# First products of an attention kernel 14 steps ahead instead of 12, and its row maxima turned three steps earlier

## The reference

```
q = x @ q_w.T + q_b
xd = depthwise conv over positions, width 3, stride 2 (2048 -> 1024), + conv_b
k = xd @ k_w.T + k_b ;  v = xd @ v_w.T + v_b
att = softmax(q k^T / sqrt(16))           # 16 heads of 16 channels, 2048 x 1024
x = layernorm(x + (att v) @ out_w.T + out_b)
x = layernorm(x + (x + 0.5 * (silu((layernorm(x)*gamma+beta) @ w1 + b1) @ w2 + b2)))
```

## Time and profile before

| | us |
|---|---|
| median of 3 runs | 5294.16 |
| lowest, highest | 5277.87, 5350.97 |
| the profiled execution | 5288.4 |
| its span, first to last instruction | 5286.6 |
| TensorE busy in the span | 4912.2 |
| VectorE, ScalarE busy | 3396.7, 2773.8 |
| mean granted TensorE clock | 0.72 of full |

### The profile page before, as it was taken

One profiled execution on the slowest core, in us unless ns is written; L12 is line 12 of the kernel. 1 busy time (PEld: TensorE's weight loads), 2 busy tenths in 40 slices (PEclk: granted clock), 3 DMA queues, 4 the chain that ended last, 5 costly groups with the idle time before them and its releaser, 6 DMA issues. The chain is left out here.

```text
span 5286.6 us, 93279 instructions
## 1 busy us (share of the span) xinstructions
PE 4912.2 (93%) x30808; PEld 2220.8 (42%) x30808; DVE 3396.7 (64%) x4144; ACT 2773.8 (52%) x4969; POOL 844.1 (16%) x553
## 2 busy tenths in 40 slices
PE   9889999999999999999899999988999998999999
PEld 6523333333333333333233333332333336999998
DVE  9765656566666566556665566565666566777775
ACT  4355555555555555555555555565555564333333
POOL 5402000000000000000000000000000005777776
PEclk9976666666765667556756566676666679999999
DMA  9921031003100400040004000400130012222221
GB/s 309 292 44 47 22 44 29 21 25 44 33 21 21 53 21 24 18 53 21 22 20 56 18 24 18 56 23 21 29 48 24 19 39 74 80 79 79 77 76 42
DMA packets 327959, 273.92 MB, mean 52 GB/s; under 512 B 170930, under 2 KB 237490, under 8 KB 327603
## 3 DMA queue, kind: packets, MB, share of 16 engines
q1 hardware_dynamic: 326482, 264.38, 20.2%
q0 software_dynamic: 1120, 4.19, 0.3%
HBM read 157.30 MB, written 110.10 MB: 51 GB/s over the span
## 5 line engine op out<-in xcount | busy, mean ns | idle before, releaser
L743 DVE TENSOR_REDUCE half_max<-first_ps 128x2 f32<-128x1024 f32 x2038 | 2489.5, 1224 | 1579.2 <-PE first_ps L592 1572.6
L709 ACT ACTIVATE probs<-score_ps 128x512 f32<-128x512 f32 x4096 | 2276.6, 597 | 1713.8 <-PE pv_ps L618 950.5
L606 PE MATMUL score_ps<-q_s,k_s 49*128 49x512 f32 x4096 | 2164.8, 614 | 318.0 <-DMA q_s<-max_row 258.3
L592 PE MATMUL first_ps<-k_s,q_s 48*128 48x512 f32 x4076 | 2089.8, 608 | 14.8 <-PEq L189 9.8
L618 PE MATMUL pv_ps<-probs,v_s 128*32 128x256 f32 x16384 | 1889.8, 547 | 1.0
L606 PEld LDWEIGHTS score_ps<-q_s,k_s 49*128 49x128 f32 x4096 | 881.8, 260 | 1736.6 <-ACT probs L709 1307.1
L592 PEld LDWEIGHTS first_ps<-k_s,q_s 48*128 48x128 f32 x4076 | 845.4, 261 | 21.6 <-issue 11.2
L618 PEld LDWEIGHTS pv_ps<-probs,v_s 128*32 128x32 f32 x16384 | 377.4, 127 | 1098.3 <-issue 686.5
L855 POOL TENSOR_TENSOR num<-num,rden 128x1024 f32<-128x1024 f32 x2 | 4.7, 2369 | 3930.2 <-DMA rden<-rden_d 3930.2
L1030 ACT ACTIVATE act_f<-fc_ps,b 128x512 f32<-128x512 f32 x256 | 174.8, 683 | 474.9 <-PE fc_ps L983 472.8
L1159 POOL TENSOR_TENSOR a_lo<-act_f,a_hi 128x512 fp32r<-128x512 f32 x256 | 338.9, 1328 | 86.9 <-DVE a_hi L1107 86.9
(11 more groups left out here) (108 smaller groups left out, 2508.6 us busy)
## 6 DMA issues: line engine op xcount, KB each, us to landing
q_s<-q_hi_d SPq DMA_DIRECT2D x512, 64.0 KB, 2.1
o_d<-o_sb SPq DMA_DIRECT2D x128, 256.0 KB, 2.0
x_t<-x_c_in SPq DMA_DIRECT2D x32, 512.0 KB, 5.6
q_hi_d<-q_hi SPq DMA_DIRECT2D x32, 512.0 KB, 4.5
q_lo_d<-q_lo SPq DMA_DIRECT2D x32, 512.0 KB, 4.9
k_s<-k_hi_d SPq DMA_DIRECT2D x128, 128.0 KB, 4.2
q_s<-q_lo_d SPq DMA_DIRECT2D x256, 64.0 KB, 2.1
q_s<-max_row SPq DMA_DIRECT2D x1024, 1.0 KB
```

The lines of the kernel that those rows point to most:

```text
L592: done = pe.matmul(first_ps[keys][:, h, :], q_s[g][at, a, t * P:(t + 1) * P], k_s[g][at, a, keys * 512:(keys + 1) * 512], start=True, stop ...
L606: pe.matmul(bank(s, u)[:, :], k_s[g][at, a, t * P:(t + 1) * P], q_s[g][at, a, :], start=True, stop=True).then_inc(scored, 1)
L709: nc.scalar.activation(probs[s % 2][:, u, :], bank(s, u)[:, :], ACT.Exp).then_inc(exped, 1)
L743: dve.reduce_max(half_max[g % 2][:, :, a * TT + t, keys], first_ps[keys][:, :, :], AX.X)\
```

## The change

Two constants. `LEAD` goes from 12 to 14: part s + 14 of the first pass runs in step s, 9 parts instead of 7 run ahead of the loop, and `again` covers 14 steps instead of 12. `TURN` gets a 1 less in its formula: with LEAD 14 it is (16 - 1 - 14) mod 8 = 1, and in step 1 part 15 is done, the last of the next group. So `rows` is called in the same step as the last maxima, directly behind the reduction that it waits for; ahead of the loop it is called with part 7 instead of part 8. The eight transfers of `load_max` stay as they are.

```
@@ -41,7 +41,7 @@
 STEPS = G * KT
-LEAD = 12
+LEAD = 14
 EARLY = 5
@@ -494,7 +494,7 @@
         FIRSTS = 2 * STEPS * NB
-        TURN = (2 * KT - LEAD) % KT
+        TURN = (2 * KT - 1 - LEAD) % KT
```

## The result

The changed kernel took 4327.16 us (median of 4 runs, 4295.69 to 4370.86); the kernel before, with one run more beside it, 5287.26 (5277.87 to 5350.97). The ratio is 0.8143, with a 95% interval from 0.8041 to 0.8246; it leaves out one execution of the changed kernel (4370.86 us) as disturbed, and so is not quite the quotient of the two medians. The changed kernel's profiled execution took 4306.35 us, span 4304.5. The forecast was 4345, between 4230 and 4520.

A forecast was written before the change was run, and what follows sets the result against it. TensorE's granted clock, mean 0.65 over the attention, was taken as the real loss, 1233 us. Attention 2560 + 108 + 70 + 431 = 3169; total 1174 + 3169 + 4 = 4347, given as 4345 us, range 4230 to 4520.

The forecast's parts named there:

- The account by clock level: Attention before the change: 2560 us of steps, 1233 lost at low clock, 258 and 36 of gaps, 4087 against 4114.
- 1024 steps at the high level: Attention: every step at granted clock 1.00, 2.50 us each, 2560 us in all.
- gaps at the loop's returns: TensorE stops at step 1 of a block at each loop return: 31 x 3.5 = 108 us.
- gaps at batch turns: At batch ends the maxima row stays late: 14 of 28 groups met at high clock, 5 us each, 70 us.
- low clock: Attention after the change: 42 falls, 24 us low each, losing 0.428 us per us, 431 us.
- Gaps lower the clock: Attention: each of 92 clock falls has a TensorE idle gap of 0.7 us or more beside it.
- The direct share of the waits: TensorE's waits for the maxima row: of 258 us, all but the batch turns' 70 us go.
- The rival that only the wait goes: Attention: the clock falls as often for another reason, only the waits are won: 5106 us, chance 0.05.
- The low stretches get shorter: Attention: low stretches average 24 us instead of 31, since very long ones crossed group turns with a late row.
- SP's queue and the batch turns: SP's in-order queue reaches load_max 16 us late at a batch's end; the earlier turn doesn't help these 28 groups.
- The lead: First products 14 steps ahead: q_s needed after ten steps, 25 us against a 16 us refill; +4 us ahead of the loop.
- VectorE's pair: VectorE's negated maxima and transpose, close together: 0.35 to 0.6 us in one piece, delay taken as 0.

The follow-up runs named there:

- lead14_turn3: The changed kernel with the square turned in step 3 of the group, first products still 14 steps ahead: 4440.88 us, ratio 0.8418 to the kernel before.
- lead12_turn3: The kernel before with only the turn moved, to step 3 behind the last maxima, first products still 12 steps ahead: 4647.43 us, ratio 0.8810.
- lead14_turn4: The changed kernel with the square turned in step 4 again, first products still 14 steps ahead: 5297.11 us, ratio 0.9953 to the kernel before.

## Why the prediction was right, point by point

**The account by clock level** carried it: shown. The attention, term by term, forecast and found in the profiled execution:

| term | forecast | found |
|---|---|---|
| 1024 steps at the high level | 2560 | 2570 at the 2.51 us of the last windows |
| gaps at the loop's returns | 108 | 80 |
| gaps at batch turns | 70 | 85 |
| low clock | 42 x 24 x 0.428 = 431 | 41 x 22.7 x 0.426 = 396 |
| attention | 3169 | 3131, by the trace 3131 |

The near hit of the sum owes something to luck: the returns cost 28 us less and the batch turns 15 us more than forecast, and the falls, 31 + 14 less three in the forecast, were 24 + 17.

**Gaps lower the clock**: shown three ways, by the row made late again (100 falls), by the gap filled (35), by the remaining gaps taken away (6). The bound drawn from the earlier trace rows, 0.7 us, is not sharp: in lead14_turn3 gaps of 0.60 us in the median (up to 1.34) left the clock alone in 78 turns, in lead12_turn3 0.97 us fells it in about half, behind a filling up to 1.54 us left it high, and in the changed kernel gaps of 1.92 and 2.02 us at two batch turns left it high. With 96 gaps in question, that ambiguity decides over 200 us, but the change skips it.

**The direct share of the waits.** Forecast 258 - 70, found 173. The rival that only the wait goes (5106) is 18% off; the time was in the clock.

**The low stretches get shorter.** I took the median of 24 for the mean of 31, because the longest had crossed turns at which the row was 0.16 us late even at the low level. The mean fell to 22.7 and the longest from 105.8 to 47.8 us. The size is right; the reason is only supported: in lead14_turn4, where the row is late again, the mean is 27.5 and the longest 71.7, yet in lead14_turn3 it is 27.2 without such a lateness in low groups. What ends a low stretch in the attention's own work stays open; seven of seven that met a filling ended in it. The prediction's "11 above 61 us" is 18 by the trace, as seven stretches are 61.4 us long; 11 are longer than that.

**SP's queue and the batch turns**: right as to place and size. The transfers that were predicted to stay late are the 20 that did, and putting them in another order took them away.

**The lead.** Its two steps need no more slack than there is: TensorE waits for q_s nowhere in the attention. Its cost ahead of the loop (+4) is +1.5: the first product with v begins at 281.19 us, not 279.66.

**VectorE's pair**, costed at nothing behind a bound of 0.35 to 0.6 us in one piece. The timeline of VectorE in the changed kernel, beside the earlier trace rows:

```profile
420.17 2.45 DVE L743 TENSOR_REDUCE half_max<-first_ps 128x2 f32<-128x1024 f32 x2 [0.17 <-PE first_ps L592]
422.65 0.19 DVE L748 TENSOR_REDUCE neg_max<-half_max 128x16 fp32r<-128x32 f32 x1
422.87 0.21 DVE L757 STREAM_TRANSPOSE max_row<-neg_max 128x32 f32<-128x32 f32 x1
423.01 17.06 DVE L743 TENSOR_REDUCE half_max<-first_ps 128x2 f32<-128x1024 f32 x14
```

From the end of the last reduction (422.62) to the start of the next 0.39 us pass, and VectorE has caught up within the 14 that follow. Right in the change; but in lead12_turn3 the same 0.4 us stood on the path of the row, and the expectation for that run left it out.

**Two small misses.** The loop of 31 iterations has 30 returns, not 31. And the sum took every return at 3.5 us; 24 met the clock high at 2.9 each, the others were mostly hidden.

## What to carry to other kernels

Where the granted clock is between its two levels while TensorE looks busy, split the stage's time by level before anything else: here 258 us of waits stood beside some 1200 us lost at the low clock. Then find the gap beside each fall (a late transfer, a queue in program order, a loop's return) and issue what it waits for earlier, or, where that can't be, try to fill it. Each that is cured lets the next one meet a high clock, so the gains do not simply add.

## What the runs showed of the hardware that was not expected

508 matmuls without a use, 487 us of them, made a kernel 12% faster. A low stretch goes on through work of the attention in which TensorE is busy for all but 2% of the time (103.29 of 105.60 us), yet each of the seven that met these matmuls ended within 5.8 us of their start. A return of TensorE's loop costs some 3 us of gap (2.9 us in the median with one block to an iteration, 4.2 at those that met the clock high with two, 2.9 with four), while the same code in a straight line shows none.
